# Six loads of 4 KB pieces for twelve of 512 bytes per attention unit, and a new order of all steps, in a transformer block on one core

## What is computed

```python
def _L0_attn_b_ref(x, wq, wk, wv, wo):
    ...
    q = (x @ wq).reshape(b, s, H, HD)          # H = 32 heads, HD = 16
    k = (x @ wk).reshape(b, s, H, HD)
    v = (x @ wv).reshape(b, s, H, HD)
    ...
    q = _apply_rotary(q, cos, sin)             # pairs (0,1), (2,3), ... of the 16 places
    k = _apply_rotary(k, cos, sin)
    scores = jnp.einsum('bqhd,bkhd->bhqk', q, k) * scale
    scores = jnp.where(causal[None, None], scores, jnp.finfo(scores.dtype).min)
    probs = jax.nn.softmax(scores, axis=-1)
    out = jnp.einsum('bhqk,bkhd->bqhd', probs, v).reshape(b, s, d)
    return out @ wo

x = x + _L0_attn_a_ref(_layernorm(x), ...)
x = x + _L0_ffn_ref(_layernorm(x), ...)
x = x + _L0_attn_b_ref(_layernorm(x), ...)
x = x + _L0_ffn_ref(_layernorm(x), ...)
```

## Time and profile before

| | us |
|---|---|
| median of 3 runs | 274.35 (273.1 to 275.1) |
| the profiled execution | 273.97 |
| its span | 272.2 |
| TensorE (PE) busy | 254.4 (93%) |
| VectorE (DVE) busy | 224.4 (82%) |
| GpSimd (POOL) busy | 182.2 (67%) |
| ScalarE (ACT) busy | 145.0 (53%) |
| DMA: 31.86 MB, packets' time as a share of 16 DMA engines | 38.8% of the span in SyncE's queue |

### The profile page before, as it was taken

The page is one execution under the profiler, slowest core; times in us unless marked ns, Lnnn a source line. Parts: engine busy times, 40 slices in busy tenths (PEclk is TensorE's granted clock), DMA queues, the critical chain, the costliest instruction groups (busy, mean ns, idle before and its releaser), DMA issues.

```text
span 272.2 us, 6539 instructions
## 1 busy us (share of the span) xinstructions
PE 254.4 (93%) x2363; PEld 213.5 (78%) x2363; DVE 224.4 (82%) x402; ACT 145.0 (53%) x239; POOL 182.2 (67%) x229
## 2 busy tenths in 40 slices
PE   7699999998989999999899999997999999999964
PEld 2597887896888987888798898885868876785744
DVE  3682679497798989899888899987988999966976
ACT  2749996644546073457443478526433683268030
POOL 5578978998798495954858587495665552475070
PEclk9999999999999999999999999999999999999999
DMA  7998170203454336334333533531634531102012
GB/s 214 294 392 297 36 198 4 77 2 94 140 147 140 92 91 168 109 88 112 103 113 108 149 94 94 146 107 45 182 111 122 158 87 52 40 3 79 31 68 98
DMA packets 51192, 31.86 MB, mean 117 GB/s; under 512 B 5400, under 2 KB 46552, under 8 KB 51160
## 3 DMA queue, kind: packets, MB, share of 16 engines
q1 hardware_dynamic: 51160, 31.44, 38.8%
HBM read 22.91 MB, written 8.39 MB: 115 GB/s over the span
## 4 chain that ended last, share of the span: by engine, by line
PE 30%; POOL 16%; SPq 15%; DVE 14%; issue 9%; ACT 8%; DMA 7%; DVEq 0%; ACTq 0%; POOLq 0%
SPq L490 13%; PE psum L885 5%; PE psum L886 5%; PE psum L887 5%; PE psum L1052 3%; POOL rstd L543 3%; DVE stats L759 3%; PE psum L1037 3%; DMA QK<-qk_parts 3%; DMA qk_parts<-parts 2%; POOL X L556 2%; DVE XT_lo L764 2%; ACT E L718 2%; PE psum L1015 2%; POOL SH L576 2%
## 5 line engine op out<-in xcount | busy, mean ns | idle before, releaser
L588 POOL TENSOR_SCALAR_AFFINE_SELECT E<-E 128x512 f32<-128x512 f32 x64 | 40.7, 661 | 36.8 <-ACT E L718 36.8
L718 ACT ACTIVATE E<-psum 128x1536 f32<-128x1536 f32 x32 | 46.4, 1449 | 26.3 <-PE psum L1039 19.5
L838 DVE TENSOR_REDUCE nmax<-psum 128x4 f32<-128x512 f32 (+1 forms) x64 | 59.1, 939 | 0.7 <-PE psum L1015 0.6
L885 PE MATMUL psum<-XT_lo,wb_hi 128*128 128x256 f32 x128 | 37.7, 294 | 0.0
L886 PE MATMUL psum<-XT_hi,wb_lo 128*128 128x256 f32 x128 | 36.2, 283 | 0.0
L887 PE MATMUL psum<-XT_hi,wb_hi 128*128 128x256 f32 x128 | 36.1, 282 | 0.0
L622 ACT ACTIVATE XN<-X,offset,rstd 128x512 f32<-128x512 f32 x30 | 24.1, 809 | 19.6 <-POOL offset L544 19.5
L764 DVE TENSOR_TENSOR XT_lo<-psum,XT_hi 128x512 fp32r<-128x512 f32 x32 | 21.5, 683 | 15.6 <-ACT XT_hi L595 15.5
L595 ACT ACTIVATE parts<-SH 128x512 bf16<-128x512 f32 x32 | 19.9, 626 | 25.4 <-POOL SH L581 14.1
L885 PE MATMUL psum<-wb_lo,XT_hi 128*128 128x256 f32 (+1 forms) x96 | 32.6, 339 | 0.0
L1015 PE MATMUL psum<-QK 128*128 128x128 bf16 x256 | 28.8, 220 | 3.1 <-DMA QK<-qk_parts 3.1
(11 more groups left out here) (104 smaller groups left out, 677.5 us busy)
## 6 DMA issues: line engine op xcount, KB each, us to landing
QK<-qk_parts SPq DMA_DIRECT2D x192, 64.0 KB
qk_parts<-parts SPq DMA_DIRECT2D x16, 384.0 KB, 2.8
X<-L_attn_a_x SPq DMA_DIRECT2D x8, 256.0 KB, 4.7
out<-X SPq DMA_DIRECT2D x6, 256.0 KB, 2.4
wb_raw<-L_attn_b_wq SPq DMA_DIRECT2D x1, 1024.0 KB, 11.0
wb_raw<-L_attn_b_wk SPq DMA_DIRECT2D x1, 1024.0 KB, 11.4
wb_raw<-L_attn_b_wv SPq DMA_DIRECT2D x1, 1024.0 KB, 11.9
QK<-mask_rows SPq DMA_DIRECT2D x8, 128.0 KB
```

Source lines behind the costliest of these rows:

```text
L588: last = nc.gpsimd.affine_select(out=e, in_=e, compare_op=ALU.is_ge, fill=0.0, base=0, pattern=[[0, GH], [1, P]], channel_multiplier=-1)
L718: nc.scalar.activation(E[:, n % 2], bank(3, 3), ACT.Exp, scale=float(HD) ** -0.5).then_inc(done[k], 1)
L838: nc.vector.tensor_reduce(nmax[:, u % 2, g::NG, t], (bank(1, 2) if t else bank(0)).rearrange("p (h k) -> p h k", h=GH), AX, ALU.max, negat ...
L885: nc.tensor.matmul(out_, stat[0], mov[1], start=first, stop=False)
```

## The change

Three things change together.

First, the columns of wq and wk are put in another order on the host, ahead of the launch: within a unit's 128 columns the order was (head, place in the head) and is now (place in the head, head). So the rotation partner lies `UH` = 8 partitions away, not 1, and the cosine and sine table is laid out to match.

Second, with that order each of the 16 places has the values of its 8 heads side by side in the scratch tensor, 8 x 256 x 2 bytes = 4 KB. `SL` reads them in 4 KB pieces, not in 512-byte pieces, and fills groups of partitions that have consecutive parts at once: `LOADS` lists the groups of 48, 32 and 16 partitions. For queries the same part is read 3, 2 and 1 times; for keys the parts 0 to n - 1 are read. So a unit has six loads and not twelve, of the same bytes.

Third, all steps stand in a new order. The list has the same 1,005 steps, none added and none taken out.

```diff
+LOADS = ((0, 3), (3, 2), (5, 1))
 KROWS = HD * len(Q_PARTS)
...
-    pair = (np.arange(P) % HD) // 2
-    sign = np.where(np.arange(P) % 2 == 0, -1.0, 1.0).astype(np.float32)
+    place = np.arange(P) // UH
+    pair = place // 2
+    sign = np.where(place % 2 == 0, -1.0, 1.0).astype(np.float32)
...
 PLAN = [
-    ("D", "x", 0, 1), ("LN", 1, 0, 1), ("D", "x", 0, 0), ("D", "x", 1, 0), ("D", "x", 1, 1), ("RS", 1, 0, 1),
...
         def stack_loads(u):
 
-            return 16 * (2 + (2 * len(Q_PARTS) + 1) * (u // QK_SLOTS) + 2 * len(Q_PARTS))
+            return 16 * (2 + (2 * len(LOADS) + 1) * (u // QK_SLOTS) + 2 * len(LOADS))
...
-                    for a, (stack, which) in enumerate(((queries(u), Q_PARTS), (keys(u), K_PARTS))):
-                        for row, c in enumerate(which):
-                            sp.dma_start(stack[row * HD:(row + 1) * HD],
-                                         scratch[u % 2, c, a].rearrange("(h d) t -> d h t", d=HD)
-                                         ).then_inc(qk_loaded[u % QK_SLOTS], 16)
+                    for row, n in LOADS:
+                        q, kk = (stack[row * HD:(row + n) * HD].rearrange("p h t -> p (h t)")
+                                 for stack in (queries(u), keys(u)))
+                        part = scratch[u % 2, Q_PARTS[row], 0].rearrange("(d h) t -> d (h t)", d=HD)
+                        sp.dma_start(q, part.unsqueeze(0).to_broadcast((n, HD, UH * S))
+                                     ).then_inc(qk_loaded[u % QK_SLOTS], 16)
+                        sp.dma_start(kk, scratch[u % 2, 0:n, 1].rearrange("c (d h) t -> c d (h t)", d=HD)
+                                     ).then_inc(qk_loaded[u % QK_SLOTS], 16)
...
-                    nc.vector.stream_shuffle(SH[:, u % 2], ps, [i ^ 1 for i in range(32)])
+                    nc.vector.stream_shuffle(SH[:, u % 2], ps, [i ^ UH for i in range(32)])
...
+    for n in ("L0_attn_b_wq", "L0_attn_b_wk"):
+        arrays[n] = np.ascontiguousarray(arrays[n].reshape(C, KT, UH, HD).transpose(0, 1, 3, 2).reshape(C, C))
```

## The result

| | before | after |
|---|---|---|
| median | 274.21 us (273.1 to 275.1) | 375.63 us (374.65 to 376.33) |
| ratio to before | | 1.370 (95% interval 1.364 to 1.376) |
| span of the profiled execution | 272.2 | 372.8 |

The account below looks back on a forecast made before the run. Before, SyncE's issuing set the loads' 8.5 us; after, DMA engines 0 and 1 would bound. 65.4 start + 217 rounds + 12.9 last load + 44.4 tail = 339.7 span, with 1.8 outside 341.5, forecast 341 us; range 303 to 368.

Parts of the forecast that it names:

- the length of a round: Cycle from one unit's loads to the next: loads 11.0, store 1.4, landing and restart 1.9, issue 0.1, together 14.4 us.
- the sentence that adds nothing for the order of the compute engines: Work queued behind TensorE's waits, projections included, runs one or two cycles ahead of its store, so 0 us was added.
- 3000 packets: Sign in the DMA view: 3000 packets under 512 B if loads use 3, 2 and 16 engines, 3864 if all use 16.
- The rival with 16 engines for all new loads: All new loads into QK spread over 16 DMA engines, hidden under issuing: 270 us (266 to 273), chance 0.12.
- The rival with other engines for each load: Few engines per load into QK, but different ones, so loads run side by side: 273 us (271 to 276), chance 0.05.
- my straight line: Line through 29 ns for 512-byte and 88 ns for 2 KB pieces, giving 167 ns per 4 KB piece on a DMA engine.
- The last load: Unit 15's loads, from their start until landed: 0.9 + 11.0 + 1.0 = 12.9 us.
- my order terms: Effects of the new order on the rounds: 2.8 for wo, +0.5 at unit 10, -1.9 at unit 11.
- the order pays: Rival: loads are fast, but the new order asks for them too soon or holds work behind `SM`: 278 us, chance 0.03.
- wo's megabyte: The load of wo now stands ahead of unit 1's loads in SyncE's queue: 2.8 us once.
- The tail: From `S` of unit 15 to the end: stays at 44.4 us, with PE busy in 38.0 of them.
- the first rival: All new loads on 16 DMA engines, taking 4 of 7.2 us of TensorE's waits: 270 us, chance 0.12.

Follow-up runs that it names:

- e1: The kernel after with its loads cut into twelve of 16 partitions, 4 KB pieces and new order kept: 288.43 us, ratio 1.053.
- e2: The kernel after with each 32-partition load cut into two of 16 partitions: 333.52 us, ratio 1.220.
- e5: The kernel after in the old order, scratch tensor rearranged so that nine loads per unit each use 16 DMA engines: 270.22 us, ratio 0.985 to before.
- e6: The kernel after in the old order, with twelve loads of 16 partitions and 4 KB pieces: 273.17 us, ratio 0.997 to before.
- e9: The kernel after in its new order, scratch tensor rearranged so that nine loads per unit each use 16 DMA engines: 270.66 us, ratio 0.990 to before.
- e4: The kernel after with its six loads per unit, but in the old order of steps: 350.67 us, ratio 1.283 to before.
- e12: The kernel after with SyncE's attention b steps in old order and `P3` of four units (`P2` of two) moved forward: 362.43 us, ratio 1.324 to before.
- e3: The kernel before, with its twelve loads of 512-byte pieces, in the new order of steps: 286.08 us, ratio 1.045.
- e10: The kernel after with only SyncE's steps of attention b put back into the old order: 375.34 us, ratio 1.371 to before.

## Why the prediction was right, and where it failed

The mechanism and the direction were right, the size was not. Two steps failed: the length of a round, where the price of a 4 KB piece was too low, and the sentence that adds nothing for the order of the compute engines.

**The DMA engines: right.** 3000 packets as worked out, and e1, e2, e5, e6 and e9 show that the time goes with the number of engines. The rival with 16 engines for all new loads, which I gave 270 us, fell; e5 and e9, which have that property with nine loads, come out at 270.2 and 270.7. The rival with other engines for each load fell as well: its loads would have landed in 7.8 us, and they take 15.

**The length of a round: the first step that failed.** A plain round takes 15.7 us for my 14.4, and over fifteen rounds that is some 20 us. Unit 4's round splits so: 1.9 us from the reset to the first large piece, 12.3 for the 66 pieces on each of the two busiest engines, 1.1 for these engines' share of the store, 0.4 to its landing. I had 11.0 for the pieces, 1.4 for the store, and 2.0 for start and landing together. The mis-sized term is the piece: 187 ns and not the 167 of my straight line, nor within its bounds of 157 to 177. Alone on their engines the pieces take 159 to 160 ns (141.5 to 147.3), so the line was close there; but in this round the first three take 1.05 us each, and those beside the 16-partition loads 300 ns on the mean (137.0 to 138.5). The last load takes 15.1 us for 12.9 by the same terms.

**The order: the second step that failed.** I wrote that what is queued on TensorE, the projections too, is "one or two cycles ahead of their store, so I add nothing for them". The projections are ahead, but the store does not hang on them alone: `P3` stands on VectorE behind work that waits for the loads. I looked at what stands behind the wait on TensorE and not at the engine that it feeds. In the kernel after this holds unit 10's loads back by 7.3 us. I had -1.4 us for the rounds from unit 9 to unit 12; they take 50.9 us, 3.8 more than three plain ones. My sum also did not see that the old order has four bursts: e4, with these, has a span of 349.7, and the order's 23 us between e4 and after are 3.5 at the start, 17.0 in the rounds, 0.8 in the last load and 1.8 in the tail, where my order terms make 1.4. e12 gives 13 of them back by `P3`; the rest is not shown step by step. In the same spirit I had made "the order pays" a rival for fast loads alone, with a chance of 0.03; e1 and e3 show it at 12 to 15 us with loads of twelve issues, and it should have been a term beside the slow loads, not instead of them.

**The smaller terms.** The start is 3.4 us later than before, for 0 in my sum. wo's megabyte: 2.8 us expected; the round from unit 0 to unit 1 takes 17.0 us, some 1.3 more than a plain one. The tail: 47.8 for 44.4, with PE busy in 42.2 of it for 38.0 at a clock of 0.95. The clock was not in my sum at all; I had read 1.00 throughout and did not ask what waits would do to it.

**Two readings.** The 7.2 us in seven waits, on which the first rival rests, count TensorE's weight loading beside its matmuls: the view of TensorE's waits before has four of the one (4.2 us) and three of the other.

```profile
PEld psum L1015 <- DMA QK<-qk_parts: 4.2, 4, 2.4
...
PE psum L1015 <- DMA QK<-qk_parts: 3.1, 3, 1.9
```

So that rival's 4 of 7.2 us was more than there is to wait, and that e5 came out at its 270 us is in part luck. And 341.5 us is the profiled execution's time; the median lies 0.4 above that, at 342 and not 341.

**The signs.** Wait for the loads in nearly every unit: 13 waits, 5.3 us on the mean, for the 3 to 5 expected. SyncE's wait for the store's landing: 92.3 us in 14 waits, 6.6 us on the mean for my 10, as part of the flight lies under its other waits. `SM`'s DMA: 10.7 us at the longest, but 3.3 in the median. DMA share in the middle: 0.26, below 0.42. Loads every 16.1 us and the last at 309.9, for 14.4 and 282. TensorE busy: 76% for 75%.

## What to carry to other kernels

Before several DMAs are merged into one, write down the outermost dimension of both sides: if they differ, as with a repeated or multi-part source, the load may run on two or three engines, and the number of completion marks among the small packets tells which. The count that fits all kernels here is the largest up to 16 that divides both. Lay the source out so that one dimension covers it (e5), and merge for the number of issues, not for the size of the pieces, where issuing sets the pace. When a transfer becomes slower, follow what waits for it through the next engine's queue up to the step that starts the next transfer; it can hold the next transfer back without any wait on the engine that the change touched (7.3 us at unit 10 here), and an order that costs nothing with short transfers (e9) can cost 25 us with long ones.

## What the hardware showed that I had not expected

- Pieces of 4 KB take 159 to 160 ns while only two or three engines carry them (141.5 to 147.3 in the kernel after), 258 to 285 on the mean when all 16 are used (e1, e6, e5), though the whole kernel moves no more than 119 GB/s on the mean.
- Loads whose sides differ in form take 0.62 to 0.77 us to issue, those of 16 partitions with one form 0.42. From the first issue to the first large piece are 1.55 us in the median round of e4 and 1.56 in that of after, and 0.94 or 0.95 in e1, e5 and e6.
- After a wait of TensorE the granted clock can stand at 0.50 (133.1 to 134.9 in the kernel after), and the same start ran at 0.69 (e12) and 1.00 (e10), with 3.3 us between them at unit 0's loads.
